# Moving a load, splitting a scaling and placing table loads in a feed-forward, attention, feed-forward kernel

## The reference, cut to what matters

```
x = layernorm(x); se = layernorm(slot_embeds) * scale          # 16 experts x 64 slots = 1024 slots
logits   = einsum("bnd,esd->bnes", x, se)
dispatch = softmax(logits, axis=1)                             # over the tokens of a batch
combine  = softmax(logits over all 1024 slots)                 # over the slots, for each token
slots = einsum("bnd,bnes->besd", x, dispatch)
eout  = (gelu(slots @ Wg + bg) * (slots @ Wu + bu)) @ Wd + bd  # for each expert, exact gelu
out   = einsum("bns,bso->bno", combine, eout)
```

## Time and profile before

| | |
|---|---|
| median of 3 runs | 1854.5 us (1850.77 to 1857.6) |
| the profiled execution, its own time | 1860.85 us |
| its span, first to last instruction | 1859.2 us |
| mean granted TensorE clock | 0.992 |
| busy: TensorE, VectorE, ScalarE, POOL | 1809.1, 1312.7, 1160.5, 823.0 us |
| expert stage of f1, of f2 | about 465 to 609, about 1511 to 1658 us |

### The profile page before, as it was taken

One profiled execution on the slowest core, in us unless ns is written; L12 is line 12 of the kernel. 1 busy time (PEld: TensorE's weight loads), 2 busy tenths in 40 slices (PEclk: granted clock), 3 DMA queues, 4 the chain that ended last, 5 costly groups with the idle time before them and its releaser, 6 DMA issues. The chain is left out here.

```text
span 1859.2 us, 35562 instructions
## 1 busy us (share of the span) xinstructions
PE 1809.1 (97%) x11756; PEld 1628.4 (88%) x11756; DVE 1312.7 (71%) x2365; ACT 1160.5 (62%) x2285; POOL 823.0 (44%) x1036
## 2 busy tenths in 40 slices
PE   7999999999999999999999999999999999999998
PEld 6788888888999999989999877888888889999998
DVE  6866666664899888845555587666565668998886
ACT  5766676675665777754444367666666755567774
POOL 3423433234778655422222134242332557885553
PEclk8999999999999999999999999999999999999999
DMA  4633343250654777712212155243423436557764
GB/s 139 249 138 146 125 158 124 103 203 24 231 184 155 252 268 268 283 47 68 68 68 68 57 226 204 108 153 147 158 91 115 158 94 222 196 181 267 264 249 150
DMA packets 106940, 297.85 MB, mean 160 GB/s; under 512 B 16784, under 2 KB 56592, under 8 KB 94544
## 3 DMA queue, kind: packets, MB, share of 16 engines
q1 hardware_dynamic: 106832, 296.49, 45.0%
HBM read 187.18 MB, written 109.28 MB: 159 GB/s over the span
## 5 line engine op out<-in xcount | busy, mean ns | idle before, releaser
L115 POOL TENSOR_TENSOR pool_carrier<-minus_half 128x1 f32<-128x1 f32 x224 | 68.9, 307 | 607.7 <-PE f1bank L984 195.5
L824 ACT ACTIVATE f2r_lt<-f2bank,slot_shift 128x512 f32<-128x512 f32 x128 | 88.3, 690 | 126.8 <-PE f2bank L955 126.7
L824 ACT ACTIVATE f1r_lt<-f1bank,slot_shift 128x512 f32<-128x512 f32 x128 | 88.4, 690 | 124.7 <-PE f1bank L955 124.6
L673 DVE TENSOR_TENSOR f2r_e_lo<-f2bank,f2r_e_hi 128x512 fp32r<-128x512 f32 x128 | 82.4, 683 | 81.1 <-ACT f2r_e_hi L905 81.1
L673 DVE TENSOR_TENSOR f1r_e_lo<-f1bank,f1r_e_hi 128x512 fp32r<-128x512 f32 x128 | 82.4, 683 | 80.4 <-ACT f1r_e_hi L905 80.4
L1693 PE MATMUL f1bank<-f1c_eo,f1c_e_hi 128*128 128x258 f32 (+1 forms) x512 | 130.6, 287 | 0.5 <-DVE f1c_xout L1599 0.4
L1693 PE MATMUL f2bank<-f2c_eo,f2c_e_hi 128*128 128x258 f32 (+1 forms) x512 | 129.9, 286 | 0.5 <-DVE f2c_xout L1599 0.4
L1694 PE MATMUL f1bank<-f1c_eo,f1c_e_hi 128*128 128x256 f32 (+1 forms) x512 | 128.1, 282 | 0.0
L1694 PE MATMUL f2bank<-f2c_eo,f2c_e_hi 128*128 128x256 f32 (+1 forms) x512 | 128.1, 282 | 0.0
L1546 POOL TENSOR_TENSOR f1c_e_lo<-f1c_lt,f1c_e_hi 128x512 fp32r<-128x512 f32 x64 | 82.8, 1296 | 76.9 <-ACT f1c_e_hi L1659 76.9
L1546 POOL TENSOR_TENSOR f2c_e_lo<-f2c_lt,f2c_e_hi 128x512 fp32r<-128x512 f32 x64 | 82.8, 1295 | 75.4 <-ACT f2c_e_hi L1659 75.4
(11 more groups left out here) (347 smaller groups left out, 6660.4 us busy)
## 6 DMA issues: line engine op xcount, KB each, us to landing
logits<-f1r_lt SPq DMA_DIRECT2D x16, 2048.0 KB, 7.4
f1c_lt<-logits SPq DMA_DIRECT2D x32, 1024.0 KB, 7.5
logits<-f2r_lt SPq DMA_DIRECT2D x16, 2048.0 KB, 7.4
f2c_lt<-logits SPq DMA_DIRECT2D x32, 1024.0 KB, 7.1
normalized<-t_xin SPq DMA_DIRECT2D x32, 512.0 KB, 2.6
t_xin<-in_L_attn_x SPq DMA_DIRECT2D x16, 512.0 KB, 5.2
f1r_xback<-normalized SPq DMA_DIRECT2D x16, 512.0 KB, 8.1
f1e_raw_g<-in_L_ffn_Wg SPq DMA_DIRECT2D x16, 512.0 KB, 4.0
```

The costliest lines, as they stand in the source:

```text
L115: pool.tensor_tensor(c["pool_carrier"][:, col:col + 1], c["minus_half"][:, 0:1], c["minus_half"][:, 0:1], ALU.add)
L673: dve.tensor_tensor(e_lo[t % 2][:, h * BANK:(h + 1) * BANK], ps_t[h][:, :], rd(e_hi[t % 2][:, h * BANK:(h + 1) * BANK]), ALU.subtract).the ...
L824: act.activation(lt[:, g, sc, :], ps_l[sc % 2][:, :], ACT.Identity, bias=c["slot_shift"][:, sc:sc + 1]).then_inc(logit_out, 1)
```

## The change

The load of the combine's first logits in SP's program is moved from the place ahead of the loop over pairs 3 to 7 to the place behind it. In the last batch, the slots of the first two experts (`FRONT = 2`) are scaled and shifted ahead of the other six of the first half, and the input parts of expert 1 are made right behind those of expert 0, no longer in the expert stage. The first weights load and the first down product wait for the new last count of the scaling. `act_table` is a small activation of one column that makes its table come in: Exp at the start of each routing, GELU at the start of the last group of the last batch.

```diff
+def act_table(act, c, function):
+    act.activation(c["pool_carrier"][:, 2:3], c["ones"][:, 0:1], function)
...
-                        for h in range(HB):
-                            if h == 0:
-                                dve.wait_ge(first_half, b)
-                            else:
-                                dve.wait_ge(dispatched, 2 + GT * (j + 1))
+                        def scale(h, begin, end):
                             for k in range(KD):
                                 dve.scalar_tensor_tensor(
-                                    out=slots[:, k, h * (E // HB):(h + 1) * (E // HB), b - 1, :],
+                                    out=slots[:, k, begin:end, b - 1, :],
...
-                            if h == 0 and fill and not exists(b, g, 1):
+
+                        dve.wait_ge(first_half, b)
+                        if fill:
+                            scale(0, 0, E // HB)
+                            if not exists(b, g, 1):
                                 exp_lo(j + 1, 0, 0)
-                            if h == 0 and not fill:
-                                experts.first_in_lo(dve)
+                        else:
+                            scale(0, 0, FRONT)
+                            experts.first_in_lo(dve)
+                            scale(0, FRONT, E // HB)
+                        dve.wait_ge(dispatched, 2 + GT * (j + 1))
+                        scale(1, E // HB, E)
...
+        act_table(act, c, ACT.Exp)
         act.sem_inc(xT_hi_done, KD)
...
+                if drain and not fill and g == NG - 1:
+                    act_table(act, c, ACT.Gelu)
...
-        for h in range(HB):
+        for n, (begin, end) in enumerate(((0, FRONT), (FRONT, E // HB), (E // HB, E))):
             for k in range(KD):
-                act.wait_ge(scaled, 3 + KD * HB * (B - 1) + KD * h + k + 1)
-                half = slots[:, k, h * (E // HB):(h + 1) * (E // HB), B - 1, :]
-                act.activation(half, half, ACT.Identity, bias=c["shift"][:, k:k + 1]).then_inc(last_slots_done, 1)
-            if h == 0:
+                act.wait_ge(scaled, 3 + KD * HB * (B - 1) + KD * n + k + 1)
+                part = slots[:, k, begin:end, B - 1, :]
+                act.activation(part, part, ACT.Identity, bias=c["shift"][:, k:k + 1]).then_inc(last_slots_done, 1)
+            if n == 0:
                 experts.first_in_hi(act)
...
     def first_in_lo(dve):
         slots_lo(dve, 0, 0)
+        slots_lo(dve, 1, 1)
...
         slots_hi(act, 0, 0)
+        slots_hi(act, 1, 1)
...
-        sp.wait_ge(route["scaled"], 3 + KD * HB * B)
+        sp.wait_ge(route["scaled"], 3 + KD * (HB * B + 1))
         emit(1, False)
...
         emit(2, False)
+        with sp.Fori(3, E // 2) as pair:
+            emit(pair, False)
         sp.wait_ge(max_stored, DMA)
         combine.load_first(sp)
-        with sp.Fori(3, E // 2) as pair:
-            emit(pair, False)
...
-        slots_hi(act, 1, 1)
...
-                if first and q == 0:
-                    slots_lo(dve, e + 1, 1 - q)
...
-        pe.wait_ge(route["scaled"], 3 + KD * HB * B)
+        pe.wait_ge(route["scaled"], 3 + KD * (HB * B + 1))
         down(0, 0, True)
```

More of the change, by code:

```diff
@@ L414, in route_stage @@
     LAST = B * NG - 1
+    FRONT = 2
     HALF = NSC // 2
@@ L780, in emit @@
                         dve.wait_ge(inv_loaded, DMA * b)
-                        for h in range(HB):
-                            if h == 0:
-                                dve.wait_ge(first_half, b)
-                            else:
-                                dve.wait_ge(dispatched, 2 + GT * (j + 1))
+                        def scale(h, begin, end):
                             for k in range(KD):
                                 dve.scalar_tensor_tensor(
-                                    out=slots[:, k, h * (E // HB):(h + 1) * (E // HB), b - 1, :],
-                                    in0=ps_s[k * HB + h][:, :].rearrange("p (e s) -> p e s", s=S),
+                                    out=slots[:, k, begin:end, b - 1, :],
+                                    in0=ps_s[k * HB + h][:, :].rearrange("p (e s) -> p e s", s=S)[:, begin - h * (E // HB):end - h * (E // HB), :],
                                     scalar=c["gain"][:, k:k + 1],
-                                    in1=inv_rows[:, h * BANK:(h + 1) * BANK].rearrange("p (e s) -> p e s", s=S),
+                                    in1=inv_rows[:, begin * S:end * S].rearrange("p (e s) -> p e s", s=S),
                                     op0=ALU.mult, op1=ALU.mult).then_inc(scaled, 1)
-                            if h == 0 and fill and not exists(b, g, 1):
+                        dve.wait_ge(first_half, b)
+                        if fill:
+                            scale(0, 0, E // HB)
+                            if not exists(b, g, 1):
                                 exp_lo(j + 1, 0, 0)
-                            if h == 0 and not fill:
-                                experts.first_in_lo(dve)
+                        else:
[4 more added lines that the diff above has]
+                        scale(1, E // HB, E)
         batches(dve, emit)
@@ L1263, in weights_hi @@
             slots_hi(act, e, q)
-        act.wait_ge(route["last_slots_done"], KD * HB)
+        act.wait_ge(route["last_slots_done"], KD * (HB + 1))
         def emit(pair, first, last):
@@ L2238, in macaron_kernel @@
         al = Scope(nc, ctx, "")
-        c = {n: al.sb(n, [P, w]) for n, w in (("ident", P), ("ones", P), ("minus_half", 8), ("dve_carrier", 1), ("pool_carrier", 2),
+        c = {n: al.sb(n, [P, w]) for n, w in (("ident", P), ("ones", P), ("minus_half", 8), ("dve_carrier", 1), ("pool_carrier", 3),
                                               ("gain", KD), ("shift", KD), ("slot_shift", NSC),
```

## The result

The changed kernel takes 1850.9 us (median of 22 runs, 1848.57 to 1853.98) against 1855.8 us (22 runs, 1850.77 to 1859.37) for the kernel before beside it: ratio 0.9977 [0.9971, 0.9983], that is 4.3 us less [3.2, 5.4]. The forecast was 1844.3 us, a gain of 10.2 us. The time lies just inside the stated range of 1840 to 1851 us, but the gain is less than half of the forecast, and it stays under the 0.5% that the prediction named as what can be told from no change.

What follows compares the result with a forecast made beforehand. TensorE, busy 97% of the span, was taken as the bound, with time to win only where it stops or runs slowly. 8.5 + 1.0 + 0.7 = 10.2 us off the median 1854.5 gave 1844.3 us, range 1840 to 1851.

Steps and rivals of the forecast that it cites:

- the first term: Logits load moved from ahead of expert 6's weights: 3.82 and 4.69 us won in the two feed-forwards, together 8.5.
- place A: Sixth expert after the first: down products 12.46 and 13.33 us apart instead of 8.64, weights late behind the logits load.
- Rival 3: The stop at place A isn't the logits' doing or returns at another expert: 1.7 us gained, 1852.8; chance 0.08.
- Place B: Border from routing to experts: front slots start TensorE 0.7 us earlier per feed-forward; plus 1.0 us in all.
- Place C: First exponentials of the second feed-forward: early Exp table removes a 1.28 us load from ScalarE's way, 0.7 us won.
- At its old place it delayed no one: Gelu table load before the change: VectorE was later, so moving it brings nothing by itself.
- rival 1: POOL holds VectorE's second subtraction in both feed-forwards, expert 2's loads late: 8.5 us gained, 1846.0; chance 0.18.
- rival 2: No hold of VectorE by POOL at the border at all: 11.8 us gained, 1842.7; chance 0.13.
- Rival 4: Slower: logits land too late at their new place, first shift waits, TensorE stops at the last expert; chance 0.04.
- Rival 5: Early Gelu load delays the group's first copies some 0.4 us per feed-forward: 9.4 us gained, 1845.1; chance 0.05.

Runs made afterwards that it cites:

- run 1: The kernel before, unchanged, one more single profiled execution: 1857.36 us.
- run 2: The kernel before, unchanged, a further single profiled execution: 1854.34 us.
- run 4: The changed kernel with the logits load back in its old place (front slots and tables only): 1856.26 us, 1.0007 of the kernel before.
- run 5: The kernel before with the front slots alone: 1858.74 us against 1857.26, ratio 1.0011.
- run 6: The kernel before with the two early table loads (Exp, Gelu) alone: 1854.41 us, 0.9989 of the kernel before.
- run 3: The kernel before with only the first logits load moved behind the loop: 1850.95 us against 1854.86, ratio 0.9979.
- first profile: The profiled execution of the kernel before that the prediction was read from: 1860.85 us, span 1859.2.
- run 9: The kernel before with only the second half of the first logits loaded behind the loop: 1851.51 us against 1857.18, ratio 0.9974.
- run 7: The changed kernel, POOL's first subtraction of up weights waiting for the low parts of both first experts: 1849.22 us against 1857.26 before, 0.9958.
- run 8: The changed kernel again, no edit, on another comparison with the kernel before: 1851.67 us against 1857.26, ratio 0.9971.
- run 10: The changed kernel with the first logits load issued behind the last two biases: 1867.89 us, 1.0060 of the kernel before.
- run 11: The kernel of run 7 measured again, no further edit: 1849.91 us against 1857.18 for the kernel before, 0.9962.
- run 12: The kernel of run 7 with expert 2's weights issued ahead of the wait for the last scaling: 1849.15 us, 0.9961 of the kernel before.
- the first repeat: Same as run 1: the kernel before, unchanged, executed once more, 1857.36 us; "the second" is run 2.

## Why the prediction was wrong

**The step that failed** is the first term, "together 8.5 us" for the logits load. It was read from one execution as if it were a constant of the kernel. The six executions with the load in its old place (in profiles of the first one and of runs 1, 2, 4, 5 and 6) show 8.5, 4.9, 3.7, 3.2, 2.2 and 2.1 us, on average 4.1; run 3 measured 3.9. With 4.1 in its place the sum is 5.8 us.

Why the size varies so. Expert 6's weights are late in all six executions, but slack swallows most of it. What is paid has three parts: the lateness beyond the slack, a hold of VectorE by POOL, and the lower clock. Both feed-forwards of the six executions (us):

| execution | feed-forward | ScalarE's wait | distance above 8.65 | TensorE's stop | VectorE's two low parts | clock fell |
|---|---|---|---|---|---|---|
| run 4 | first | 3.64 | 0.26 | none | 0.75 | no |
| run 6 | first | 4.05 | 0.67 | 0.43 | 0.75 | no |
| run 2 | first | 4.20 | 0.83 | 0.59 | 0.75 | no |
| run 1 | first | 4.39 | 1.02 | 0.78 | 0.75 | no |
| run 5 | first | 4.58 | 1.19 | 0.95 | 0.75 | no |
| first profile | first | 4.86 | 3.81 | 2.08 | 1.59 | yes |
| run 5 | second | 4.43 | 1.03 | 0.80 | 0.75 | no |
| run 6 | second | 4.81 | 1.43 | 1.19 | 0.75 | no |
| run 2 | second | 4.89 | 2.88 | 2.64 | 1.59 | no |
| run 4 | second | 5.50 | 2.97 | 2.73 | 1.59 | no |
| run 1 | second | 4.65 | 3.91 | 2.39 | 1.59 | yes |
| first profile | second | 5.23 | 4.68 | 2.97 | 1.59 | yes |

In the first five rows the cost is the wait less 3.4 us. In the sixth the same rule gives 1.46. The hold of 0.84 us (1.59 instead of 0.75) comes on top, then about 1.5 us for the clock, which makes 3.8. All five stops of 2 us and more are those with the hold, and the clock fell only after three of these, for 1.3 to 1.5 us (the prediction had 1.7). The hold comes with the lateness: where the weights are late enough, TensorE has finished its down product before POOL is through with the low part of Wu, and POOL's L1153 arrives 0.06 to 0.08 us behind VectorE's start. In the other seven it comes 0.4 us or more behind, and in six of these POOL is seen to wait for the down product first.

So the 8.5 us of the first profile are, as an estimate from these rows, 3.8 of lateness, 1.7 of two holds and 3.0 of two falls of the clock. The average of 4.1 is 2.7, 0.7 and 0.7. The prediction saw the hold at 514.78 and the clock, and took both for what happens every time. It carried the total of this execution down by 6.3 us to the median and left the stall in it at its full size. An execution 6.3 us above the median was a warning that one of its stalls was larger than usual: the six spans lie between 1851.4 and 1859.2 us, and without the cost of place A between 1848.9 and 1850.8.

**Place A, the mechanism**: right. The distances fell to 8.7 to 9.2 us, the clock stayed at 1.00, and ScalarE's wait for expert 6 fell to 1.63 and 1.52 us. The new place costs nothing: the logits landed ahead of the first shift, as worked out. A distance of 9.16 us stays in the second feed-forward, and of 9.22 in run 3, which has no front slots; in both ScalarE waits 3.4 us for weights one expert earlier, and why these are late wasn't looked into. Rival 3 (not the logits' doing) is out by runs 3, 4 and 9.

**Place B**: 1.0 us was forecast, the middle between a hold in both feed-forwards and none. It came in one of the two: first low parts and TensorE 0.7 us earlier in each; no hold in the first; in the second the hold leaves expert 1 about 0.6 us earlier (0.8 forecast), and experts 2 and 3 lose 0.2 + 0.6 us, behind weights issued at 1510.77, 5.4 us behind the first hidden product where before it was 1.5 (0.5 forecast). By stage lengths that is about 0.5 us won in place of 1.0. But the middle wasn't a chance between two outcomes. In all five executions with the front slots and without run 7's edit (after, runs 4, 5, 8 and 10) POOL came in between in the second feed-forward, 1.26 to 1.28 us behind VectorE's start, and not in the first, at 1.57 to 1.58. Before the change too POOL's L1247 came 0.3 us later in the first, 1.20 us behind VectorE's start against 0.90 in the earlier trace rows. The rows of the first:

```profile
464.21 0.76 DVE L1186 TENSOR_TENSOR f1e_in_lo<-f1r_slots,f1e_in_hi 128x256 fp32r<-128x256 f32 x2 [1.51 <-ACT f1e_in_hi L1180]
...
465.41 2.41 POOL L1247 TENSOR_TENSOR f1e_lo_u<-f1e_raw_u,f1e_hi_u 128x1024 fp32r<-128x1024 f32 x1 [1.63 <-DVE f1e_in_lo L1186]
```

The prediction took the 0.14 us between the low parts and POOL from the second feed-forward for both. Why POOL is later in the first stays open.

**Place C**: right in the Exp table's 0.7 us. "At its old place it delayed no one" was true of the old order alone: run 5 shows that the front slots need the early Gelu table. The two edits were costed apart, and they belong together.

**The sum.** By stage lengths 4.1 + 0.5 + 0.7 = 5.3 us, against 4.3 [3.2, 5.4] in the comparison and 5.4 (0.9971) in run 8's. By the same measure 0.5, 0.6 and 0.1 us of place A are still there in the kernel after, run 3 and run 8, so about 5 is the better sum. Run 4 shows no gain, with at most 0.9 us by its interval, where 0.5 + 0.7 = 1.2 would be expected. Its own trace accounts for most of that. The two expert stages, from first hidden to last down product and without place A, take 284.1 us together, where the four executions with the old border (the first profile, runs 1, 2 and 6) take 281.9 to 282.5 and the kernel after 283.1. So 1.4 us won ahead of the borders and 0.7 by the table meet some 1.8 lost behind them, in distances of 8.86 to 9.20 us. Why these were longer than in the kernel after stays open. The stretch from the last down product of the first feed-forward to the first logits product of the second routing, which no edit touches, differs between executions by 3 us (460.0 to 462.9 us), so a single profile can't settle a microsecond, and I didn't measure those two edits with more runs. That the front slots and the tables gain anything in time is therefore not shown.

**Rivals 1 and 2**: the kernel after has rival 1's hold in the second feed-forward and rival 2's free border in the first, each time. Run 7 forces the case of rival 2, and the medians of runs 7, 11 and 12, 7.3 to 8.0 us below the kernel before, are the best of the study. **Rival 4** is a real danger with the wrong first user: the small load of row maxima is read 3 us ahead of the first shift, and I had looked at the logits alone. **Rival 5** didn't occur.

## What to carry to other kernels

Before a stall is priced, look at the same place in several executions: where a late transfer is mostly swallowed by slack, a few tenths more of lateness can bring in a hold by another engine and a fall of the clock, and one profile can show twice the usual cost. Look for the same meeting of engines in both halves of the kernel too: here it came out differently in each, and the same way every time. If the profiled execution lies above all the timed ones, cut its stalls, not only its total. And when an edit moves work ahead of a border, list what else sits between the border and the first result (here a table load, a POOL subtraction and a queue's wait), for the gain ends at the next of them.

## What the runs showed of the hardware

The granted clock doesn't fall after every stop of the same length. In the first repeat TensorE stopped for 2.39 us and the next matmul took 0.58 us instead of 0.38; in the second it stopped longer, 2.64 us, and went on at full clock. Timeline of TensorE and a window of 1 us behind the stop, first repeat, then second:

```profile
1562.02 0.58 PE L1352 MATMUL f2bank<-f2e_in_hi,f2e_hi_g 128*128 128x256 f32 x1 [2.39 <-DVE f2e_in_lo L1186]
...
1563.00:1564.00 1.00, 1.00 (x7) 1.00 (x6) 1.00 (x1) 0.77 (x2) 1.00 (x2) 0.50 0.00 0
```

```profile
1560.09 0.38 PE L1352 MATMUL f2bank<-f2e_in_hi,f2e_hi_g 128*128 128x256 f32 x1 [2.64 <-DVE f2e_in_lo L1186]
...
1561.00:1562.00 1.00, 1.00 (x11) 1.00 (x10) 1.00 (x1) 0.85 (x3) 1.00 (x1) 1.00 0.00 0
```

After the stops of 2.08 and 2.97 us in the first profile it fell too; after one of 2.73 us in run 4 it didn't, nor after those up to 1.19 us at the same place. What decides among the stops above 2 us stays open.

VectorE and POOL excluded each other for the whole of an instruction in the meetings looked at here. POOL's subtraction of 2.45 us, arriving among VectorE's four, made them 4.00 us instead of 1.80, and POOL's L1153 of 1.23 to 1.26 us, arriving between the two of place A, made them 1.59 instead of 0.75. A difference of 0.3 us in POOL's start decides. At the border it came out the same way in all five executions, at place A it went with the lateness of the weights.
